# Attention scores from two float16 parts, two heads in the row halves of the array, and the router product with its operands exchanged

## The reference

```python
h = mfcc(x) @ w_proj + b_proj                       # (16, 750, 192)
hn = layernorm(h)
q, k, v = hn @ V_Q @ U_Q + bias_q, ..., ...         # 12 heads of 16
qm, km = einsum("bhsd,dr->bhsr", q, M_U), einsum("rd,bhtd->bhrt", M_V, k)
attn = softmax(einsum("bhsr,bhrt->bhst", qm, km) / sqrt(16))   # 750 x 750 for each head
h = h + (attn @ v)
x2 = layernorm(h)
scores = softmax(x2 @ gate_w.T)                     # the router, 8 experts
w, idx = top-2 of 8, from the best 2 of 4 groups by scores + gate_b
out = h + sum_e w_e * (swiglu((x2 @ W1_e + B1_e) * (x2 @ W3_e + B3_e)) @ W2_e + B2_e) + the shared expert
```

## Time and profile before

| | |
|---|---|
| median of 3 runs | 3468.13 us (3450.93 to 3470.53) |
| the profiled execution | 3472.8 us, of which the span of its instructions is 3470.9 |
| mean granted TensorE clock | 0.922 |
| TensorE busy | 3234.6 us (93%) |
| VectorE busy | 2154.5 us (62%) |
| ScalarE busy | 1664.3 us (48%) |
| GpSimd busy | 629.5 us (18%) |
| the FFN of one batch, in the middle of the run | 68.20 us, TensorE busy 67.56, clock 1.00 |

### The profile page before, as it was taken

The page is one execution under the profiler, slowest core; times in us unless marked ns, Lnnn a source line. Parts: engine busy times, 40 slices in busy tenths (PEclk is TensorE's granted clock), DMA queues, the critical chain, the costliest instruction groups (busy, mean ns, idle before and its releaser), DMA issues.

```text
span 3470.9 us, 56629 instructions
## 1 busy us (share of the span) xinstructions
PE 3234.6 (93%) x22736; PEld 1849.6 (53%) x22736; DVE 2154.5 (62%) x3828; ACT 1664.3 (48%) x2403; POOL 629.5 (18%) x1097
## 2 busy tenths in 40 slices
PE   6888999999999999999999999999999999999987
PEld 3454455464655546464554546455554645555555
DVE  3317666666766666666666666676666657667545
ACT  1133644545454454546455454545545454545542
POOL 1520120303012030301203030221203021120201
PEclk8657989998998989999999989999998999989889
DMA  5324320312122130312212031222203121221000
GB/s 124 113 90 100 78 42 14 80 29 77 23 69 37 39 67 17 77 22 69 37 55 54 14 77 27 70 35 60 46 14 77 32 74 25 62 37 26 8 7 7
DMA packets 146214, 174.55 MB, mean 50 GB/s; under 512 B 30081, under 2 KB 134874, under 8 KB 143950
## 3 DMA queue, kind: packets, MB, share of 16 engines
q1 hardware_dynamic: 143772, 163.37, 19.8%
q0 software_dynamic: 1280, 7.08, 0.9%
q10 hardware_dynamic: 898, 0.47, 0.1%
HBM read 105.49 MB, written 64.51 MB: 49 GB/s over the span
## 4 chain that ended last, share of the span: by engine, by line
PE 71%; DVE 13%; ACT 7%; issue 4%; SPq 2%; DMA 2%; POOL 1%; ACTq 0%; DVEq 0%; POOLq 0%
PE ps L1109 69%; DVE negm L920 6%; ACT big L738 2%; DVE st L864 2%; ACT hn L703 1%; PE ps L1278 1%; ACT rest L670 1%; PE ps L1195 1%; ACT parts L686 1%; DVE mpart L927 1%; SPq L383 1%; DVE onrm L951 1%; DVE rest L1024 1%; POOL h0t L493 0%; DVE mvr L870 0%
## 5 line engine op out<-in xcount | busy, mean ns | idle before, releaser
L920 DVE TENSOR_REDUCE negm<-ps 125x1 f32<-125x750 f32 x1152 | 1065.4, 935 | 618.9 <-PE ps L1109 608.5
L738 ACT ACTIVATE big<-ps 125x750 f32<-125x750 f32 x1152 | 906.3, 793 | 770.3 <-PE ps L1109 766.5
L1109 PE MATMUL ps<-qs,ks 99*125 99x375 bf16 x2304 | 658.6, 370 | 57.5 <-DVE negm L920 49.7
L1109 PE MATMUL ps<-ks,qs 96*125 96x375 bf16 x2304 | 627.8, 357 | 56.0 <-ACT big L738 22.2
L1109 PE MATMUL ps<-big,V 125*32 125x188 f32 (+1 forms) x9216 | 625.1, 353 | 2.8 <-ACT big L738 0.4
L1109 PEld LDWEIGHTS ps<-qs,ks 99*125 99x125 bf16 x2304 | 243.9, 144 | 415.8 <-issue 238.4
L1024 DVE SCALAR_TENSOR_TENSOR rest<-ps,fb,h1s 128x375 f32<-128x375 f32 (+1 forms) x448 | 251.7, 603 | 321.8 <-PE ps L1109 320.5
L1109 PEld LDWEIGHTS ps<-ks,qs 96*125 96x125 bf16 x2304 | 310.6, 148 | 218.3 <-issue 68.4
L1109 PEld LDWEIGHTS ps<-big,V 125*32 125x32 f32 x9216 | 200.6, 111 | 329.3 <-issue 319.2
L493 POOL TENSOR_TENSOR h0t<-h0t,onrm 125x384 f32<-125x384 f32 x48 | 48.0, 1001 | 1796.7 <-DVE onrm L951 1796.4
L752 ACT ACTIVATE h1s<-ps,fb,wsc 128x375 f32<-128x375 f32 (+1 forms) x448 | 272.0, 657 | 211.7 <-PE ps L1109 211.7
(11 more groups left out here) (173 smaller groups left out, 3333.7 us busy)
## 6 DMA issues: line engine op xcount, KB each, us to landing
qs<-qk_scratch SPq DMA_DIRECT2D x288, 93.8 KB, 3.6
ks<-qk_scratch SPq DMA_DIRECT2D x288, 93.8 KB, 4.6
qk_scratch<-parts SPq DMA_DIRECT2D x32, 562.5 KB, 4.8
v_scratch<-vtmp SPq DMA_DIRECT2D x16, 1125.0 KB
V<-v_scratch SPq DMA_DIRECT2D x48, 375.0 KB
h_scratch<-h0t SPq DMA_DIRECT2D x16, 562.5 KB
hn<-h_scratch SPq DMA_DIRECT2D x16, 562.5 KB
h0t<-h_scratch SPq DMA_DIRECT2D x16, 562.5 KB
```

The lines of the kernel that those rows point to most:

```text
L738: nc.scalar.activation(halves(probs[:, i % 2, h, :]), slot(s, TP), ACT.Exp).then_inc(exp_done, 1)
L920: V_.tensor_reduce(negm[:, n:n + 1], slot(s, TP), axis=AX.XY, op=MAX, negate=True).then_inc(max_done, 1)
L1109: return nc.tensor.matmul(o, l, r, start=start, stop=stop)
```

## The change

1. q and k are split into two float16 parts. Three products of parts, 3 x 16 = 48 rows, replace the six of 96; two rows of maxima replace three. For range, the weights of q and k are scaled by powers of two in the setup, and the exponential undoes that by its scale.
2. The stacks hold two heads: one in rows 0 to 47 (49 with the maxima), the other in rows 64 to 111 (113). The two matmuls of an A or B tile are now those of two heads for one half of the columns, one in each row half of the array. VectorE takes two maxima from an A tile (over X instead of XY), and `max_parts` combines the two column halves. The number of tiles, matmuls and columns is the same.
3. A q/k tile: ScalarE writes the first part straight from PSUM, VectorE subtracts from PSUM into the second part, and the slot is free after that (`parts_ready`) instead of after the raw copy. ScalarE's second-part pass and GpSimd's third-part pass are gone.
4. The router: the 8 weight columns are stationary and x2 moves (ten matmuls with 375 columns into 8 rows), ScalarE copies the 8 x 750 logits, and six transposes turn them (a fourth F tile). F tiles 2 and 3 stand after B tiles 18 and 20; F tile 2 stood after B tile 19.
5. DMAs: four for the max rows of a group instead of three, stacks of half the bytes in as many DMAs as before. In the setup: maxima of wq and wk and scaling with them, memsets, own buffers for the staged FFN weights.

```diff
-SLOTS = 6
-QPARTS = ((0, 3, 0), (3, 2, 1), (5, 1, 2))
-KPARTS = ((0, 3), (3, 2), (5, 1))
+QPARTS = (0, 0, 1)
+KPARTS = (0, 1, 0)
+SLOTS = len(QPARTS)
 KROWS = SLOTS * D
-MROWS = 3
+MROWS = 2
+HP = HG // 2
-PREP_AFTER = {14: (0, 1), 19: (2,)}
+PREP_AFTER = {14: (0, 1), 18: (2,), 20: (3,)}
...
-            return (raw_ready, 4 * m + k - 1) if k < 6 else (v_ready, 3 * m + k - 5)
+            return (parts_ready, 4 * m + k - 1) if k < 6 else (v_ready, 3 * m + k - 5)
...
-                for c in range(3):
-                    dst = qs[KROWS + c:KROWS + c + 1, g, :].rearrange("o (r t) -> o r t", r=TILES)
-                    sp.dma_start(dst, mTs[TILES * c:TILES * c + TILES, :]).then_inc(maxrows_loaded[g], 16)
+                for q in range(2):
+                    for c in range(MROWS):
+                        r0, n = TILES * c + HP * J * q, HP * J
+                        dst = qs[64 * q + KROWS + c:64 * q + KROWS + c + 1, g, :].rearrange("o (r t) -> o r t", r=n)
+                        sp.dma_start(dst, mTs[r0:r0 + n, :]).then_inc(maxrows_loaded[g], 16)
...
-                    wait(act, parts_ready, 4 * m + t - 1)
-                    nc.scalar.activation(halves(rest[0:rows, t % 2, :]), slot(s, rows), ACT.Copy).then_inc(raw_ready, 1)
                     if t == 0:
                         wait(act, parts_stored, 64 * m)
-                    act.wait_ge(raw_ready, 4 * m + t + 1)
-                    nc.scalar.activation(parts[0:rows, t, 0, :], rest[0:rows, t % 2, :], ACT.Copy).then_inc(part1_ready, 1)
+                    nc.scalar.activation(halves(parts[0:rows, t, 0, :]), slot(s, rows), ACT.Copy).then_inc(part1_ready, 1)
...
-            def pre_rest(m, t):
+            def pre_rest(m, t, s):
                 rows = 128 if t % 2 == 0 else E - 128
-                r_ = rest[0:rows, t % 2, :]
                 dve.wait_ge(part1_ready, 4 * m + t + 1)
-                V_.tensor_tensor(r_, r_, parts[0:rows, t, 0, :], op=SUB).then_inc(rest_ready, 1)
+                hi, lo = (parts[0:rows, t, c, :].rearrange("p (n c) -> p n c", n=2) for c in range(2))
+                V_.tensor_tensor(lo, slot(s, rows), hi, op=SUB).then_inc(parts_ready, 1)
...
-                V_.tensor_reduce(negm[:, n:n + 1], slot(s, TP), axis=AX.XY, op=MAX, negate=True).then_inc(max_done, 1)
+                V_.tensor_reduce(negp[:, 2 * n:2 * n + 2], slot(s, TP), axis=AX.X, op=MAX, negate=True).then_inc(max_done, 1)
...
-                    for j in range(J):
-                        c = slice(TP * j, TP * j + TP)
-                        o = ps[0:TP, 2 * s, NX * j:NX * j + NX]
-                        mm(o, x2Ah[:, c], gwh[:, 0, :], True, False)
...
+                    for q in range(2):
+                        t = slice(HC * q, HC * q + HC)
+                        o = slot(s, NX)[:, q, :]
+                        mm(o, gwh[:, 0, :], x2Ah[:, t], True, False)
...
+                    pe.wait_ge(gate_copied, m + 1)
                     for j in range(J):
...
+                        ins = nc.tensor.transpose(ps[0:TP, 2 * s, NX * j:NX * j + NX], lT[:, TP * j:TP * j + TP], idf[0:NX, 0:NX])
+                    ins.then_inc(gate_turned, 1)
...
-                h, j = n // J, n % J
+                c, j, n2 = n // (2 * J), n % (2 * J) // 2, n % 2
                 for q in range(2):
-                    ins = mm(slot(s, TP)[:, q, :], qs[0:KROWS, g, NF * h + TP * j:NF * h + TP * j + TP],
-                             ks[0:KROWS, g, NF * h + HC * q:NF * h + HC * q + HC])
+                    r = slice(64 * q, 64 * q + KROWS)
+                    ins = mm(slot(s, TP)[:, q, :], qs[r, g, NF * c + TP * j:NF * c + TP * j + TP],
+                             ks[r, g, NF * c + HC * n2:NF * c + HC * n2 + HC])
```

More of the change, by code:

```diff
@@ L69, in schedule @@
             tiles += [("P", i, pre) for i in PRE_AFTER.get(k, ())]
-    assert len(tiles) % 3 == 0
-    return tiles
+    return tiles + [None] * (-len(tiles) % 3)
 def first_schedule():
@@ L208, in build @@
         scratch = parts[:].rearrange("p t c n -> p (t c n)").bitcast(fp32)
-        wst = [qs[:].rearrange("p g c -> p (g c)").bitcast(fp32)[:, 2 * NFF * i:2 * NFF * i + 2 * NFF] for i in range(2)]
+        sel_s = hn2[0:4 * NE1].rearrange("p j e -> p (j e)")[:, 0:CH * 128]
+        wst = [wst0[:], wst1[:]]
         def tmp(rows, n):
@@ L379, in load_stacks @@
                 h0 = g * HG * D
[L380 to L387, removed]
+                for i, (stack, order) in enumerate(((ks, KPARTS), (qs, QPARTS))):
+                    for q in range(2):
+                        for s, part in enumerate(order):
+                            src = qk_dram[bass.ds(m, 1), 1 - i, part, h0:h0 + HG * D, :].rearrange("o (c r d) t -> (o r) d c t", r=2, d=D)[q]
+                            dst = stack[64 * q + D * s:64 * q + D * s + D, g, :].rearrange("p (c t) -> p c t", c=HP)
+                            sp.dma_start(dst, src).then_inc(stacks_loaded[g], 16)
                 if g == 0:
@@ L513, in pre_norm @@
                 ins.then_inc(ln1_ready, 1)
-            def third_parts(m):
-                for t in range(4):
-                    rows = 128 if t % 2 == 0 else E - 128
-                    pool.wait_ge(part2_ready, 4 * m + t + 1)
-                    P_.tensor_tensor(parts[0:rows, t, 2, :], rest[0:rows, t % 2, :], parts[0:rows, t, 1, :], op=SUB).then_inc(parts_ready, 1)
             def fold(dst, src, n):
@@ L681, in pre_tile @@
                     nc.scalar.activation(vtmp[:, 2 * q:2 * q + 2, :, 0:D], src, ACT.Copy).then_inc(v_ready, 1)
-            def second_part(m, t):
-                rows = 128 if t % 2 == 0 else E - 128
-                act.wait_ge(rest_ready, 4 * m + t + 1)
-                nc.scalar.activation(parts[0:rows, t, 1, :], rest[0:rows, t % 2, :], ACT.Copy).then_inc(part2_ready, 1)
             def prep_tile(m, i, s):
@@ L696, in prep_tile, with copy_logits @@
                 nc.scalar.activation(hi[:], raw[:], ACT.Copy).then_inc(x2hi_ready, 1)
+            def copy_logits(m, s):
+                act.wait_ge(gate_done, m + 1)
+                wait(act, gate_turned, m)
+                nc.scalar.activation(halves(lT[:]), slot(s, NX), ACT.Copy).then_inc(gate_copied, 1)
             def ffn_apply(m, step):
@@ L789, in _ @@
                 prep_tile(B - 1, i, i)
+            copy_logits(B - 1, 2)
             gate_exp(B - 1)
@@ L999, in att @@
                             max_parts(3 * b + g + 1)
-                    if kind == "F" and k == 2:
+                    if kind == "F" and k == 3:
                         ffn_logits(b - 1, s)
```

150 lines of the change are left out of this document (83 added, 67 removed).

## The result

The changed kernel takes 3760.98 us (median of 4 runs, 3744.26 to 3773.42) where the kernel before took 3469.33 beside it: a ratio of 1.0846, 95% interval 1.0784 to 1.0909. The forecast was 3342, between 3220 and 3530: faster was forecast, and it is slower. The profiled execution has a span of 3742.4 us and a mean granted clock of 0.782, where it was 0.922.

A forecast was written before the change was run, and what follows sets the result against it. TensorE was taken as the bound nearly everywhere. Terms of −3.8, −3.0, +0.6 and −2.9 gave −9.1 us a batch; with batches 0, 14, 15 and start-up −126, from 3472.8 to 3347, at the median 3342 us (3220 to 3530).

The forecast's parts named there:

- Group 2 (53.10 us, clock 1.00): Attention with projections of batch b + 2: plain pairs gain, q/k waits cost 0, shape changes about 0.6; −2.9 us a batch.
- The score tiles: A and B matmuls: row halves run at once, a pair takes 0.95 us for 1.24, or 1.62 for 2.22 at 1.2 GHz.
- Rival (c): Score tiles: the row halves don't run at once, pairs stay at 1.24 us; about 3430 us, chance 0.08.
- Group 0: Attention with FFN preparation, 43.70 us: faster pairs, less four more pairs falling to 1.2 GHz in the middle; −3.8 us a batch.
- Group 1: Attention of 34.50 us: the fall at its start goes; 27.0 if it stays at 2.4 GHz; −3.0 us a batch over three cases.
- falls halfway: Group 1 case: clock drops midway, 12 pairs at 1.12 and 12 at 1.62 us, 33 us, −1.5; weighted one quarter.
- FFN: Unchanged stretch: its first 3.4 us slow if group 1 ends at 1.2 GHz, one case in three; +0.6 us a batch.
- (b): Thinner scores hold TensorE at 1.2 GHz from mid group 0 through group 1: 3510 us, 3580 if group 2 half falls; chance 0.25.
- (a): The clock never falls in attention, wide router and faster pairs keeping TensorE full: −17 us a batch, about 3225; chance 0.12.
- (d): VectorE or the ring of three slots becomes the bound: pairs stop at about 1.1 us, about 3410 us; chance 0.13.

The follow-up runs named there:

- The kernel with the wait filled: Changed kernel plus 18 extra matmuls nobody reads ahead of each wait for a q/k tile's slot, four times a batch: 3431.91 us, ratio 0.9915 to the kernel before.
- the longer wait in the kernel before: Kernel before, with a q/k tile's slot counted as free only when VectorE has subtracted, not after ScalarE's raw copy: median 3698.88 us.
- the zero rows: Changed kernel with score matmuls widened to 62 (A) and 64 (B) rows in each half, the added rows holding zeros: 3341.34 us, ratio 0.9619 to the kernel before.
- the raw copy: Changed kernel with q/k slots freed as before by ScalarE's copy into SBUF, VectorE subtracting in SBUF: 3353.18 us, ratio 0.9643 to the kernel before.
- both remedies: Changed kernel with score rows filled up with zeros and q/k slots freed by ScalarE's raw copy: 3246.09 us, ratio 0.9365 to the kernel before.

## Why the prediction was wrong

**The step that failed** is "Group 2 (53.10 us, clock 1.00)": it costed the wait for the subtraction, between −0.6 and +0.3 us for each of four tiles, and took the clock of before for granted. The wait was found and placed rightly (1.12 us on TensorE, from the subtraction behind a maximum), but its price is the clock that it brings down. Group 2 came to 73.10, at a clock of 0.63, instead of 50.2: 22.9 of the 31.5 us a batch that lie between −9.1 forecast and +22.4 measured. The kernel with the wait filled takes 52.90 although the slot comes no earlier, so 20.2 of these are clock; the longer wait in the kernel before shows that a wait is enough alone at 96 rows, and the zero rows show that the thin scores make the clock give way more easily. The forecast did let idle time bring the clock down in the middle of group 0, but not here.

**The score tiles.** A pair takes 0.92 where 0.95 was taken, and 1.60 at the lower level, where 1.62 was taken. Rival (c) is out. The mechanism was right; groups 0 and 2 gained from it only once the clock was up.

**Group 0** was to gain 3.8 and came to 43.80 for 43.70. The forecast had four pairs more at 1.2 GHz; in fact the clock came in low from group 2 of the batch before and stayed low until 1762.9. **Group 1:** 36.10 for a forecast of 31.5; the changed kernel is the case "falls halfway", put at 33, in eleven batches. That the wide router keeps its beginning at 1.00 was right, and with full rows and the raw copy it takes 29.60 (27 was taken for this case). **FFN:** +0.7 for +0.6 is luck. The forecast had its first 3.4 us slow in one case of three; they are in eleven batches of the changed kernel, and the FFN of batch 5 in the kernel before happened to be longer than that of batch 6 (68.20 and 67.60).

**The router.** Worth 79 us alone in the kernel before, nothing beside both remedies, and in the changed kernel its undoing made things 45 us faster. What it is worth depends on how long the clock stays low behind it in each company.

**Rivals.** (b), with a quarter of the chance, came nearest: a clock held down makes the kernel slower. But it named the thin scores alone, not the wait, and saw the start in the middle of group 0, which is where the clock comes back in the changed kernel (and where the raw copy alone leaves 0.91). Its price was less than a quarter of the real one: it let group 2 fall for half its pairs and charged 4.5 us for that, counting plain pairs at 1.62 and leaving the q/k tiles at their price of 2.4 GHz, although they lengthen too (from one to the next 9.43 us for 5.88). Its 3580 lay outside the range that was stated, and the measured time lies beyond both. (a) came nearest to what the two remedies give, 3246 for 3225, but that is another kernel. (d) is out: VectorE's idle time grew.

The Trainium skill ("TensorEngine Tiling (Array Packing)", PSUM Bottleneck) says that tiling speeds up TensorE but not the draining of PSUM, which may then become the bound. The kernel with both remedies agrees in part: in its group 1 of 29.60 us VectorE is busy in 24.59 and TensorE, busy in 26.02, waits 2.6 for the row maxima.

## What to carry to other kernels

Where TensorE's clock moves, a wait has two prices: its own length, and that of everything behind it at half speed. So cost a new wait on TensorE with the clock that the stretch may lose, matmuls of every kind included, before believing a gain that makes TensorE's work shorter. Here it paid to let the first engine that can copy a slot of PSUM free it, not the last one that needs it (3353 us for 3761), and to pad matmuls that need few rows with zero rows, which cost no stream time (0.37 us for a tile of 48 and of 62 rows alike).

## What the runs showed of the hardware that was not expected

The granted clock answers to rows that only multiply by zero: 48 and 50 rows in each half against 62 and 64, with the same columns, order and waits, gave a mean clock of 0.782 and 0.942. It answers to work that nobody reads: 18 matmuls of 128 x 128 in a wait, 0.782 against 0.889, and 329 us. And streams as long as before with half the rows (0.686) did worse than half as long with two halves at once (0.782). None of this is a rule: the same instructions are followed by a fall in some batches and not in others (4 of 13 with the zero rows). Two matmuls in the two row halves run together in 0.37 us, the length of each.
